# Moving a two-element copy and a clamp of the gating step from VectorE to GpSimd, and splitting the step over three slots

## The reference, cut to what matters

```python
x = x + 0.5 * ffn(layernorm(x))
x = x + attn(layernorm(x))
x = x + 0.5 * ffn(layernorm(x))
```

```python
logits = normalize(flat) @ normalize(sim_matrix, 0) - sigmoid(gates)
gated = relu(logits)
mask = gated > 0                       # straight-through estimator left out
inactive = sum(mask, axis=1) == 0
_, fb_idx = top_k(logits, 2)           # fallback: the two best experts
mask = where(inactive & is_in(fb_idx), 1.0, mask)
rw = softmax(where(mask > 0, gated, -inf))
```

## Time and profile before

| what | value |
|---|---|
| median of 3 runs | 4348.94 us (4347.72 to 4352.06) |
| the profiled execution's own time | 4347.72 us |
| its span, first to last instruction | 4345.9 us |
| DVE busy | 4053.9 us (93%) |
| PE busy | 3835.5 us (88%) |
| POOL busy | 3624.5 us (83%) |
| ACT busy | 3577.5 us (82%) |
| mean granted TensorE clock | 0.949 of full speed |

### The profile page before, as it was taken

How to read it: one execution, slowest core, us unless ns; L and a number is a source line. 1 busy time by engine, 2 the same in 40 slices (tenths; PEclk the granted TensorE clock), 3 DMA queues, 4 the chain that set the end, 5 groups by cost and what they waited for, 6 DMA issues and landing times.

```text
span 4345.9 us, 93568 instructions
## 1 busy us (share of the span) xinstructions
PE 3835.5 (88%) x29004; PEld 3138.4 (72%) x29004; DVE 4053.9 (93%) x14267; ACT 3577.5 (82%) x9797; POOL 3624.5 (83%) x4170
## 2 busy tenths in 40 slices
PE   6777889998999999899999999989999999987777
PEld 5556777777777777777777777777777777765666
DVE  2389999999999999999999999999999999999992
ACT  2378989888898988889898888989888888888772
POOL 1467999999999999999999999999999999976660
PEclk8878999999999999999999999999999999999788
DMA  3111112221212112121212112121212212110011
GB/s 103 43 33 34 52 54 58 55 56 54 59 55 56 56 53 58 54 59 55 57 54 56 55 55 58 55 58 51 60 53 56 58 53 58 53 47 23 28 33 54
DMA packets 243941, 230.47 MB, mean 53 GB/s; under 512 B 27123, under 2 KB 176628, under 8 KB 243316
## 3 DMA queue, kind: packets, MB, share of 16 engines
q1 hardware_dynamic: 243444, 224.49, 18.9%
HBM read 214.98 MB, written 9.44 MB: 52 GB/s over the span
## 4 chain that ended last, share of the span: by engine, by line
DVE 67%; PE 12%; POOL 11%; ACT 7%; issue 2%; DMA 1%; SPq 0%; ACTq 0%; POOLq 0%; DVEq 0%
DVE M L989 12%; DVE HL L991 10%; DVE HL L1006 5%; DVE HL L1014 5%; DVE HL L1020 5%; DVE HL L1010 5%; PE pQ L653 4%; DVE M L1008 4%; DVE M L1022 4%; DVE M L1004 4%; DVE HL L1012 4%; DVE M L1018 4%; DVE HL L1016 4%; POOL HS L401 3%; POOL S L1074 2%
## 5 line engine op out<-in xcount | busy, mean ns | idle before, releaser
L653 PE MATMUL pQ<-wf_sb,HS 128*128 128x192 f32 x8192 | 1477.7, 335 | 90.6 <-POOL HS L401 67.1
L653 PEld LDWEIGHTS pQ<-wf_sb,HS 128*128 128x128 f32 x8192 | 1377.9, 196 | 131.1 <-issue 112.4
L885 ACT ACTIVATE S<-S,M 128x512 f32<-128x512 f32 x1024 | 802.4, 784 | 6.3 <-DVE M L989 3.4
L892 ACT ACTIVATE S<-S,lift 128x512 f32<-128x512 f32 x1024 | 789.2, 771 | 2.3 <-POOL lift L1063 2.3
L401 POOL TENSOR_TENSOR HS<-hT_a,RB 128x1024 f32<-128x1024 f32 x244 | 578.1, 2369 | 0.1
L401 POOL TENSOR_TENSOR HS<-hT_b,RB 128x1024 f32<-128x1024 f32 x240 | 568.2, 2368 | 5.2 <-PE pQ L653 3.4
L880 ACT COPY PTs<-pST 128x512 f32<-128x512 f32 x1024 | 529.1, 614 | 5.0 <-PE pST L672 4.7
L672 PE MATMUL pST<-ident,S 128*128 128x128 f32 x4096 | 509.9, 280 | 17.1 <-ACT S L868 12.4
L1072 POOL TENSOR_TENSOR HL<-S,HL 128x512 f32<-128x512 f32 x384 | 491.6, 1280 | 34.6 <-ACT HL L873 34.1
L1074 POOL TENSOR_TENSOR S<-HL 128x512 f32<-128x512 f32 x384 | 493.7, 1286 | 30.1
L672 PEld LDWEIGHTS pST<-ident,S 128*128 128x128 f32 x4096 | 475.8, 145 | 32.8 <-ACT S L868 13.6
(11 more groups left out here) (255 smaller groups left out, 8748.7 us busy)
## 6 DMA issues: line engine op xcount, KB each, us to landing
RB<-rows_b SPq DMA_DIRECT2D x384, 256.0 KB, 3.4
RB<-rows_a SPq DMA_DIRECT2D x384, 256.0 KB, 3.4
x_b<-in_x SPq DMA_DIRECT2D x64, 128.0 KB, 3.1
out_y<-y SPq DMA_DIRECT2D x64, 128.0 KB, 1.7
wf_sb<-in_wf SPq DMA_DIRECT2D x4, 768.0 KB, 6.9
rows_b<-rwT SPq DMA_DIRECT2D x64, 8.0 KB, 1.3
wof_sb<-in_wof SPq DMA_DIRECT2D x1, 1024.0 KB, 7.3
rows_a<-rwT SPq DMA_DIRECT2D x64, 8.0 KB, 1.3
```

Source lines behind the costliest of these rows:

```text
L653: mm = nc.tensor.matmul(pQ[:, 0:QKV], HS[:, k % 2, e, i, :], wf_sb[:, i, at:at + QKV], start=k + e + i == 0, stop=(k, e, i) == (3, 3, 1))
L885: nc.scalar.activation(S[:, r, :], S[:, r, :], ACT.Prelu, bias=M8[:, r, TH:TH + 1], scale=-1.0, alpha=1.0 / STEEP).then_inc(s_cut, 1)
L892: nc.scalar.activation(S[:, r, :], S[:, r, :], ACT.Exp, bias=lift[:, r:r + 1], scale=-STEEP).then_inc(s_gap, 1)
```

## The change

The four instructions of the step "top" are taken apart. VectorE keeps MAX8 in slots 3 and 9. The copy of the two largest becomes a step of its own, "pair", which is a job's small step and so GpSimd's (VectorE's for the tiles at the ends): slot 4 for a, slot 10 for b. MATCH_REPLACE becomes the step "repl" on VectorE in slot 5 for a and 11 for b. The bias nv is no longer a reduction on VectorE but a fifth instruction of the step "gate", max with 0 and times -1, on GpSimd. The gate's semaphore counts to five in a tile, so the exponential waits for all five. The buffer v8 is 8 wide instead of 16, and one memset at the start is gone.

```diff
-        "hT": 79, "h_rinv": 79, "lg": 81, "shift": 82, "top": 83, "gate": 87,
+        "hT": 79, "h_rinv": 79, "lg": 81, "shift": 82, "top": 83, "pair": 84, "repl": 85, "gate": 87,
...
-        "lg": -41, "shift": -40, "top": -39, "gate": -34, "gate_exp": -33,
+        "lg": -41, "shift": -40, "top": -39, "pair": -38, "repl": -37, "gate": -34, "gate_exp": -33,
...
+            if at := mine("pair"):
+                t, c = at
+                wait(eng, q["top"], t + 1)
+                ns.tensor_copy(J.mr8[:, 0:2], J.v8[:, 0:2]).then_inc(q["pair"], 1)
             if at := mine("gate"):
...
                 if ends:
-                    wait(eng, g, 4 * t)
+                    wait(eng, g, 5 * t)
...
                 ns.tensor_scalar(J.pos[:], J.L[:], 0.0, None, ALU.is_gt).then_inc(g, 1)
-                wait(eng, g, 4 * t + 3)
+                ns.tensor_scalar(J.nv[:], J.v8[:, 0:1], 0.0, -1.0, ALU.max, ALU.mult).then_inc(g, 1)
+                wait(eng, g, 5 * t + 4)
...
-                    nc.vector.max(J.v8[:, 0:8], J.L[:]).then_inc(q["top"], 1)
-                    dve.wait_ge(q["top"], t + 1)
-                    nc.vector.tensor_reduce(J.mr8[:, 0:2], J.v8[:, 0:2].unsqueeze(2), mybir.AxisListType.X, ALU.max
-                                            ).then_inc(q["pair"], 1)
-                    nc.vector.tensor_reduce(J.nv[:], J.v8[:, 0:16:8], mybir.AxisListType.X, ALU.max, negate=True
-                                            ).then_inc(q["guard"], 1)
-                    dve.wait_ge(q["pair"], t + 1)
+                    nc.vector.max(J.v8[:], J.L[:]).then_inc(q["top"], 1)
+                if at := tile(J, "repl", w, j):
+                    t, c = at
+                    wait(dve, q["pair"], t + 1)
                     nc.vector.match_replace(J.R[:], J.mr8[:], J.L[:], -BIG).then_inc(q["repl"], 1)
```

More of the change, by code:

```diff
@@ L257, in __init__ @@
                     sb(f"{k}_{n}", P, E) for k in ("Lr", "L", "R", "fb", "fb2", "pos", "ep", "eg", "em", "rw"))
-                self.v8 = sb(f"v8_{n}", P, 16)
+                self.v8 = sb(f"v8_{n}", P, 8)
                 self.mr8 = sb(f"mr8_{n}", P, 8)
@@ L271, in __init__ @@
                     "full", "read", "x_in", "x_sum", "x_sq", "x_eps", "x_rstd", "x_bias", "h_norm", "h_sq",
-                    "h_guard", "h_rinv", "shift", "top", "pair", "guard", "repl", "gate", "gate_exp", "gate_em", "gate_sum",
+                    "h_guard", "h_rinv", "shift", "top", "pair", "repl", "gate", "gate_exp", "gate_em", "gate_sum",
                     "gate_rec", "rw", "rw_st", "sc_max", "sc_exp", "sc_rec", "sc_norm")}
@@ L382, in layer @@
                 ns.tensor_tensor(J.ep[:], J.eg[:], J.pos[:], ALU.mult).then_inc(q["gate_em"], 1)
-                wait(eng, q["gate"], 4 * t + 4)
+                wait(eng, q["gate"], 5 * t + 5)
                 eng.wait_ge(q["gate_em"], 2 * t + 1)
@@ L735, in ffn @@
                     t, c = at
-                    act.wait_ge(q["gate"], 4 * t + 4)
+                    act.wait_ge(q["gate"], 5 * t + 5)
                     nc.scalar.activation(J.eg[:], J.L[:], ACT.Exp, bias=J.nv[:]).then_inc(q["gate_exp"], 1)
@@ L936, in _ @@
                 nc.vector.memset(jobs[n].mr8[:], BIG)
-                nc.vector.memset(jobs[n].v8[:], 0.0)
             nc.vector.memset(keep[:, 0:1], 0.0)
```

## The result

The changed kernel takes 4585.1 us (median of 4 runs, 4581.81 to 4590.6) against 4349.49 us of the kernel before, a ratio of 1.0543 with a 95% interval of 1.0524 to 1.0561. The forecast was 4569 us.

What follows compares the result with a forecast made beforehand. VectorE was taken as the bound. Delay of 12.6 us and clock of 1.6 us a sequence gave 192 us over 54 turns; with 28 at the ends, 4347.7 became 4568, as median 4569 us; 8 in 10 range 4410 to 4650.

Steps and rivals of the forecast that it cites:

- What bounds the kernel, and the lead: VectorE is the bound; GpSimd reaches slot 4 3.06 to 4.42 us before MAX8 of a ends and will stand still.
- The path from the stop to nm_a: GpSimd's delay passes through RB2, TensorE and ScalarE to VectorE's nm_a: 12.03 us a sequence, 12.6 with MATCH_REPLACE of b.
- TensorE's clock: Longer idle time ahead of the eight matmuls lowers TensorE's clock: 1.6 us a sequence, between 0 and 4.
- slack of 0.28 at HS of b: Turn 1: TensorE alone would be 3.51 us late, GpSimd's HS of b 3.79; the difference swallows little of the clock's cost.
- the ends: Last ten turns, without job b: 2.8 us each, bounds 0 and 7, 28 us; before 384 us nothing.
- One bound: GpSimd's added copy: at most 0.55 us, since no small instruction there is longer from start to start; 0.20 taken.
- The saving on VectorE: Slot 3's group on VectorE shrinks by 0.30 us per tile, 38 us at most, vanishing in nm_a's wait.
- Only the splits bite: Rival, 0.12: ScalarE and TensorE make up their delay before slot 11; only lo in slot 10 stops VectorE; 4417 us.
- It grows: Rival, 0.10: nothing absorbs the delay, 4.57 us in each turn, and the clock falls in each, 1.16; 4694 us.

Runs made afterwards that it cites:

- e1: The changed kernel with the copy of the two largest one slot later on GpSimd, slot 5 for a and 11 for b; 4342.35 us, ratio 0.9978.
- e2: The kernel before, with GpSimd only made to wait in slot 4 for job a's MAX8, nothing moved; 4548.83 us, ratio 1.0461.
- e8: The changed kernel with the copy behind the product HS of its slot instead of ahead of it, both jobs; 4449.93 us, ratio 1.0230.
- e3: The changed kernel with 20 small filler transposes on TensorE in slot 6 ahead of the wait for RB2; 4511.92 us, ratio 1.0371.
- e6: The kernel before with filler transposes on TensorE ahead of the wait for RB2, in turns 1 to 3; 4334.78 us, ratio 0.9963.
- e5: e1 with filler transposes on TensorE ahead of the wait for RB2, in turns 1 to 3; 4311.5 us, ratio 0.9912 against the kernel before.
- e4: The kernel before with only the bias nv moved to GpSimd's gate step; 4348.55 us, ratio 0.9994.
- e7: The changed kernel with job a's copy alone moved to slot 5, job b's left in slot 10; 4338.48 us, ratio 0.9971.

## Why the prediction was right, and where a size was off

*What bounds the kernel, and the lead.* Right. The copy waits 272.6 us for MAX8 of a, some 270 were forecast; 4.33, 4.39, 4.36 and 3.21 us in turns 1 to 4 against leads of 4.36, 4.42, 4.37 and 3.06. Held up by e1, where the same copy in a place that GpSimd reaches after MAX8 costs nothing, and by e2, where the wait without the copy costs 4.6%.

*The path from the stop to nm_a.* Right as a mechanism. RB2 begins 2130.38 - 2122.60 = 7.78 us after MAX8, which were 3.26 before: 4.52 late, forecast 4.56. e8 shows the same reckoning with half the lead. Turn by turn without the clock the forecast was 12.6 us a sequence. The delay's own part is the changed kernel with its clock kept up (e3) against the kernel before with its clock kept up (e6): 262.32 - 250.50 = 11.8 us in the sequence of the table, and (3540.5 - 3384.5) / 13.5 = 11.6 over all 54 turns. That the sum is so near is in part luck. By turns it is 2.4, 2.6, 3.8 and 3.1 us where 2.3, 3.5, 4.7 and 2.1 were forecast: two turns 0.9 too high and one 1.0 too low. (e6 has no filler in turn 4; its eight matmuls took 1.97 us there anyway.)

*TensorE's clock.* The term that was mis-sized. I took 1.6 us a sequence between ends of 0 and 4; the whole addition of 17.1 less 11.8 leaves 5.3 in this sequence, and 16.0 - 11.6 = 4.4 over the 54 turns, beyond the upper end. The step that failed was the price of one fall. I took the 1.16 us that turn 2 showed for the eight matmuls; with the longer idle time the clock is low through all eight and into the scores: 3.75 - 1.97 and 1.80 - 1.14, together 2.44 us in turn 1. The slack of 0.28 at HS of b, on which I relied there, is small against that: TensorE's L658 for b begins 24.52 us after MAX8 instead of 18.78, 5.7 late, and GpSimd's own HS of b is 4.38 late instead of 3.79, because L_b now waits 0.52 us for a result that passed TensorE. So the delay was partly carried by TensorE, not by GpSimd as I had it, and turn 1 lost 4.5 instead of 2.3 to 3.2 us. Turn 4 lost 3.8 instead of 2.1 to 3.3; there the eight matmuls took 2.64 us.

*How near the number came.* The median came 16 us above the forecast and the traced execution 20, less than the errors in the sum. Over the 54 turns the delay's part was 156 us and not 170, the clock's 60 and not 22, and the ends took 24 and not 28: the clock was 38 us too low, and the other two took back 18 of them.

*The other terms.* Turn 2 lost 3.4 us (forecast 3.5, its clock was already low). The last turns lost 2.2 us each over seven of them, 2.8 forecast; the last 130 us lost 8 us more. At 384 us the changed kernel was 0.6 us behind, and before that never more than 1.4. One bound was misread: of GpSimd's small instructions one takes 0.67 us to the next start and none was said to take more than 0.55; nothing hangs on it, the copy took 0.15.

*The saving on VectorE.* 0.30 us a tile, right (e5), and worth nothing in the changed kernel, as forecast; its busy time in the sequence fell by 1.28 us, 0.16 a tile, and where the rest went is not shown. The row behind MAX8, in turn 1 of the changed kernel:

```profile
2122.68 0.53 DVE L970 TENSOR_REDUCE nm_b<-Sr 128x1 f32<-128x384 f32 x1
```

It starts 0.08 us after MAX8 at 2122.60; with an instruction behind it that waited for its result that was 0.20, and I had taken 0.09. By the rule of the Trainium skill (VectorE: DVE Perf Modes, "The DRAIN you can't avoid") it would have stayed at 0.20 and 0.19 us a tile would have been saved; the 0.08 and e5's 0.30 speak against its use here.

*The rivals.* "Only the splits bite" was half there: lo makes VectorE wait 1.85 us in turn 1, but nm_a's wait behind it covers it. Of "It grows" one half came, the clock that falls in turns 1 and 4 too; the other half, that nothing takes up the delay, did not. Why e4's and e6's gains are 5 us off what their waits say isn't settled; both are near the limit of the measurement. An earlier MAX8, in slot 1, with the copy left in slot 4, was not run.

## What to carry to other kernels

Before an instruction is moved to another engine, look at when that engine gets to its new place and when its input is ready: here a copy of 0.15 us from the bound engine went to one that was 4.4 us ahead, and that engine's lead was what fed everything else. One slot later the same copy is free. And where a stop lengthens TensorE's idle time, count the matmuls behind it at the lower clock; a few dummy matmuls in an idle time that can't be avoided were worth 0.4% in the kernel before (e6), 0.7% on top of the late copy (e5 against e1), and 1.7% in the disturbed one (e3).

## What the runs showed of the hardware

The low clock is not a matter of the length of the idle time alone. Idle times of 2.17 us (e2, turn 4) and 2.58 us went by without a fall, one of 2.30 us did not; after 4.64 us all eight matmuls ran at 0.51; and in e1 three groups of matmuls took 1.2 us longer behind one of 3.02 us than behind one of 2.88 us in the kernel before. In e7 one of 3.04 us went by without a fall:

```profile
2404.30 1.97 PE L602 MATMUL pFa<-wof_sb,RB 128*128 128x256 f32 x8 [3.04 <-POOL RB L419]
```

Nor does a turn have its own price. In the changed kernel the eight matmuls of turn 1 took 3.75 us behind 4.64 us idle, and one sequence later, again 10.27 us after MAX8, 1.97 us:

```profile
2395.00 5.49 PE L658 MATMUL pQ<-wf_sb,HS 128*128 128x192 f32 x16 [2.17 <-POOL HS L406]
2402.51 1.97 PE L602 MATMUL pFa<-wof_sb,RB 128*128 128x256 f32 x8 [2.03 <-POOL RB L419]
```

There the low clock fell on the sixteen matmuls ahead of the wait, which took 5.49 us behind 2.17 us idle, where they took 2.87 behind 2.16 in turn 1. They ran into time in which TensorE would have waited for RB2 anyway, the idle time shrank to 2.03 us, and the turn lost 2.4 us instead of 4.5. So what a fall costs depends on which matmuls it meets, those ahead of the wait or those behind it. The turns of one sequence in the table show where the clock costs, and only the sum over many sequences what it costs. The Trainium skill (TensorE: Matmul & The Clock Gate, "What's actually happening") calls the ramp variable from run to run; the trace shows that it is variable within a run too.
